# Flamingo block, gated cross attention and MoLE feed-forward: the rest of the values in 32x32 tiles, the last maxima on another engine, the score steps in another order

## The reference

```python
def xattn(query, ctx):                       # 16 heads of 16 channels
    q = (query @ Wq.T + bq) * 16 ** -0.5
    k, v = ctx @ Wk.T + bk, ctx @ Wv.T + bv
    q, k, v = split_heads(q), split_heads(k), split_heads(v)
    k, q = xpos_apply(k, downscale=True), xpos_apply(q, downscale=False)
    w = softmax(einsum('btd,bsd->bts', q, k))          # over 154 keys
    return join_heads(einsum('bts,bsd->btd', w, v)) @ Wo.T + bo

def mole(x, W, b, A, Bm, Rw):                # 3 experts of rank 8
    gates = softmax(x @ Rw)
    return x @ W + b + 1 / 8 * sum_e((x @ A[e]) * gates[e] @ Bm[e])

x = x + tanh(g_xattn) * xattn(layernorm(x), ctx)
x = x + tanh(g_ffn) * mole(relu(mole(layernorm(x), W1, ...)), W2, ...)
```

## Time and profile before

| | |
|---|---|
| median of 3 runs | 531.51 us (530.65 to 532.06) |
| the profiled execution | 530.21 us, of it the span of the trace 528.4 us |
| busy: TensorE / VectorE / ScalarE / GpSimd | 92% / 72% / 39% / 13% |
| mean granted TensorE clock | 0.963 of 2.4 GHz |
| exponentials (L625) | 80 of 1.03 us, 80.6 us |
| values (L1310) and their rest (L1302) | 256 and 64 records on TensorE |

### The profile page before, as it was taken

How to read it: one execution, slowest core, us unless ns; L and a number is a source line. 1 busy time by engine, 2 the same in 40 slices (tenths; PEclk the granted TensorE clock), 3 DMA queues, 4 the chain that set the end, 5 groups by cost and what they waited for, 6 DMA issues and landing times.

```text
span 528.4 us, 7891 instructions
## 1 busy us (share of the span) xinstructions
PE 486.6 (92%) x3032; PEld 353.5 (67%) x3032; DVE 380.0 (72%) x896; ACT 205.3 (39%) x325; POOL 70.5 (13%) x118
## 2 busy tenths in 40 slices
PE   4449939999999999999999999999999999999997
PEld 3335336847876597847876597847876597748796
DVE  4746586958897697958897697958897687925543
ACT  6333522571227412571227412571227412460320
POOL 6363020020202011020202011020202010020000
PEclk9956977999999999999999999999999999999999
DMA  8461140106002140207102140206002040200011
GB/s 320 130 204 43 40 122 2 37 18 190 17 1 82 41 122 1 78 18 186 20 1 82 41 122 1 81 14 189 17 1 82 1 122 1 78 5 1 1 42 40
DMA packets 20385, 34.30 MB, mean 65 GB/s; under 512 B 5588, under 2 KB 9500, under 8 KB 20220
## 3 DMA queue, kind: packets, MB, share of 16 engines
q1 hardware_dynamic: 12704, 16.28, 11.2%
q10 hardware_dynamic: 7644, 17.52, 10.4%
HBM read 14.28 MB, written 4.19 MB: 35 GB/s over the span
## 4 chain that ended last, share of the span: by engine, by line
PE 77%; DVE 14%; ACT 3%; issue 2%; DMA 2%; POOL 1%; SPq 1%; ACTq 0%; DVEq 0%
PE psF L1228 17%; PE psF L1191 13%; PE psX L1211 7%; PE psO L1310 5%; PE psX L1287 4%; PE psX L1118 4%; PE psX L1101 4%; PE psX L1282 4%; PE psF L1302 3%; PE psO L1302 3%; DVE max_t L832 3%; PE psF L1197 3%; DVE xT_lo L765 2%; PE psF L1064 1%; PE psX L1191 1%
## 5 line engine op out<-in xcount | busy, mean ns | idle before, releaser
L832 DVE TENSOR_REDUCE max_t<-psX 128x4 fp32r<-128x616 f32 x128 | 98.9, 795 | 13.1 <-PE psX L1211 11.5
L1211 PE MATMUL psX<-km,qT 128*128 128x308 f32 x256 | 65.6, 346 | 15.8 <-DMA qT<-probs 10.9
L1228 PE MATMUL psF<-w_hi,h_hi 128*128 128x284 f32 (+1 forms) x240 | 72.5, 302 | 0.1
L1228 PE MATMUL psF<-w_lo,h_hi 128*128 128x284 f32 (+1 forms) x240 | 70.3, 293 | 0.0
L1228 PE MATMUL psF<-w_hi,h_lo 128*128 128x284 f32 (+1 forms) x240 | 70.1, 292 | 0.0
L1211 PEld LDWEIGHTS psX<-km,qT 128*128 128x128 f32 x256 | 48.0, 206 | 32.0 <-DVE max_t L832 12.0
L625 ACT ACTIVATE probs<-psX 128x1024 f32<-128x1024 f32 x64 | 64.2, 1025 | 10.9 <-PE psX L1287 10.6
L543 ACT ACTIVATE h_hi<-psF 128x512 fp32r<-128x512 f32 x59 | 34.4, 595 | 55.9 <-PE psF L1197 55.9
L1228 PEld LDWEIGHTS psF<-w_hi,h_hi 128*128 128x128 f32 x240 | 45.1, 188 | 6.0 <-issue 6.0
L402 POOL TENSOR_TENSOR x<-x,tab 128x256 f32<-128x256 f32 x32 | 22.3, 726 | 183.1 <-DMA x<-in_x_dram 183.1
L825 DVE SCALAR_TENSOR_TENSOR h_lo<-psF,h_hi 128x512 fp32r<-128x512 f32 x59 | 39.7, 683 | 8.0 <-ACT h_hi L543 8.0
(11 more groups left out here) (170 smaller groups left out, 881.2 us busy)
## 6 DMA issues: line engine op xcount, KB each, us to landing
qT<-probs SPq DMA_DIRECT2D x32, 256.0 KB
qT<-probs ACTq DMA_DIRECT2D x16, 256.0 KB
x<-in_x_dram ACTq DMA_DIRECT2D x8, 512.0 KB, 3.4
x_ln<-in_x_dram ACTq DMA_DIRECT2D x7, 512.0 KB, 4.1
out_dram<-x ACTq DMA_DIRECT2D x7, 512.0 KB, 2.9
turn<-in_turns_dram SPq DMA_DIRECT2D x2, 512.0 KB, 6.7
heads_t<-in_w_dram SPq DMA_DIRECT2D x1, 1024.0 KB, 8.3
heads_t<-in_w_dram SPq DMA_DIRECT2D x1, 994.0 KB, 7.0
```

Source lines behind the costliest of these rows:

```text
L832: V.tensor_reduce(max_t[:, k, half, :].rearrange("p (h g) -> p g h", h=2)[:, 2 * j:2 * j + 2, :], psX[:, 2 * j:2 * j + 2, 0:2 * S].rearran ...
L1211: ins = mm(psX[:, g % 4, 0:2 * S].rearrange("p (h s) -> p h s", h=2), qT[:, g, tokens(k)], km[:, g, :, 0:S], start=True, stop=True)
L1228: ins = mm(out_bank(d, k)[:, cs], a[:, m, tokens(k)], w[:, m, cs], start=m == 0 and i == 0, stop=m == HT - 1 and i == 2)
```

## The change

- `vr_sb` shrinks from 128 x (4 x 128) to 128 x (4 x 32). `values_rest(c, pair)` now issues eight matmuls of 32 rows x 32 columns: for each of four blocks, the two groups r of the pair, each with its own 32 partitions of `probs_r` and `vr_sb`. `place(r, block)` gives the 32 columns, so that the eight lie in eight different tiles; group 2 pair goes to `psO`, group 2 pair + 1 to a bank of `psF`. The heads are dealt to the groups in another order (`MAIN_PAIRS`, `perm_v` on the host).
- The second rest step of the scores stands fourth (i = 3); both halves of the maxima are waited for by then. `values_rest(c, 0)` waits for four exponentials, part 1 of the values for six.
- `scores(c, 0)` is issued in two halves, with `max_transposed(c, 1)` between. The 16th `max_scores` stands inside `hidden_main(d, 7)`, and VectorE takes the 16th maximum ahead of `h_low(d, 5)`.
- ScalarE copies both halves of the maxima; one DMA for each half.
- `xT_high` stands behind exponential 3 in place of 2, `ctx_copy` behind 6 in place of 4. `project_k` moves from behind score step 7 to behind part 2 of the values, ahead of step 9.
- `project_v` computes for each block of rest values only its own 64 columns.

```diff
-        vr_sb = sb("vr_sb", [P, NQ, P])
+        vr_sb = sb("vr_sb", [P, 4, 32])
...
-                    for hh in range(2):
-                        sp.dma_start(qT[HR * hh + KM:HR * hh + KM + 1, 4 * f:4 * f + 4, :].bitcast(F32),
-                                     max_f[4 * hh:4 * hh + 4, f, :].bitcast(F32)).then_inc(max_rows[f].sem, 16)
+                    sp.dma_start(qT[KM::HR, 4 * f:4 * f + 4, :].bitcast(F32),
+                                 max_f[:, f, :].bitcast(F32)).then_inc(max_rows[f].sem, 16)
...
+                maxima_copy(c, 1)
                 for i, (kind, n) in enumerate(SCORE_STEPS):
...
-                    if i == 2 and not last:
+                    if i == 3 and not last:
                         xT_high(c + 1)
-                    if i == 4 and not last and u == 1:
+                    if i == 6 and not last and u == 1:
                         ctx_copy(b + 1)
...
-                        h_low(d, m)
+                        if m == HT - 2:
+                            h_low(d, m - 1)
+                        if m != HT - 3:
+                            h_low(d, m)
...
-                dve.wait_ge(maxT_ps.sem, maxT_ps.at(c))
-                V.tensor_scalar(max_f[:, 1, :], psO[0:H // 2, :], -1.0, None, ALU.mult).then_inc(maxT_s[1].sem, 1)
...
-                        ins = mm(psF[32 * j:32 * j + SR, 2, E:2 * E], ctxT[:, f, P:S], wkv_sb[:, f, E:2 * E],
+                        o = E + 4 * D * j
+                        ins = mm(psF[32 * j:32 * j + SR, 2, E:E + 4 * D], ctxT[:, f, P:S], wkv_sb[:, f, o:o + 4 * D],
...
+            def place(r, block):
+                return (block + 2 * (r % 2)) % 4
...
-            def values_rest(c, g, first, last):
-                pe.wait_ge(sc_exp.sem, sc_exp.at(c, (1, 1, 6, 6)[g]))
...
-                mm(pv_bank(g), vr_sb[:, g, :], probs_r[:, g, :], start=True, stop=False)
+            def values_rest(c, pair, first, last):
+                pe.wait_ge(sc_exp.sem, sc_exp.at(c, 4))
+                if pair == 1:
+                    pe.wait_ge(pv_t.sem, pv_t.at(c, 1))
...
+                for block in range(4):
+                    for r in (2 * pair, 2 * pair + 1):
+                        j, rows = place(r, block), slice(32 * r, 32 * r + 32)
+                        mm(pv_bank(r)[32 * j:32 * j + 32, :], vr_sb[rows, j, :], probs_r[rows, block, :],
+                           start=pair == 1 or block >= 2, stop=pair == 0 and block < 2)
...
-                pe.wait_ge(sc_exp.sem, sc_exp.at(c, (3, 5, 8, 10)[part]))
+                pe.wait_ge(sc_exp.sem, sc_exp.at(c, (3, 6, 8, 10)[part]))
...
-                scores(c, 0)
+                scores(c, 0, (0, 1))
                 max_transposed(c, 1, first)
+                scores(c, 0, (2, 3))
                 scores(c, 1)
...
                 scores(c, 2)
-                values_rest(c, 0, first, last)
                 scores(c, 3)
-                values_rest(c, 1, first, last)
+                values(c, 0, first)
                 scores(c, 4)
-                values(c, 0)
+                scores(c, 5)
+                values_rest(c, 0, first, last)
+                scores(c, 6)
                 if u == 1 and not last:
                     ctx_transposed(b + 1, ctx_sb)
-                scores(c, 5)
-                scores(c, 6)
                 values(c, 1)
                 scores(c, 7)
+                scores(c, 8)
+                values_rest(c, 1, first, last)
+                values(c, 2)
                 if u == 1 and not last:
                     project_k(b + 1)
-                scores(c, 8)
-                values_rest(c, 3, first, last)
                 scores(c, 9)
-                values_rest(c, 2, first, last)
-                values(c, 2)
...
-SCORE_STEPS = [("rest", 0), ("main", 0), ("main", 2), ("main", 4), ("main", 6),
-               ("rest", 2), ("main", 8), ("main", 10), ("main", 12), ("main", 14)]
+SCORE_STEPS = [("rest", 0), ("main", 0), ("main", 2), ("rest", 2), ("main", 4), ("main", 6),
+               ("main", 8), ("main", 10), ("main", 12), ("main", 14)]
+MAIN_PAIRS = (0, 1, 4, 5, 2, 3, 6, 7)
```

More of the change, by code:

```diff
@@ L218, in build @@
         maxT_ps = count("maxT_ps", 2)
-        maxT_s, max_rows = ([count(f"{n}{f}", per) for f in range(2)] for n, per in (("maxT_s", 1), ("max_rows", 32)))
+        maxT_s, max_rows = ([count(f"{n}{f}", per) for f in range(2)] for n, per in (("maxT_s", 1), ("max_rows", 16)))
         sc_ps, sc_exp = count("sc_ps", 10), count("sc_exp", 10)
@@ L510, in key_constants @@
                     rows = slice(HR * hh, HR * hh + HR)
-                    copy(rest_blocks(rows, hh), one[hh][rows].to_broadcast([HR, NG, SR])).then_inc(kr_init.sem, 1)
+                    copy(rest_blocks(rows), one[hh][rows].to_broadcast([HR, NG, SR])).then_inc(kr_init.sem, 1)
             def key_high(b):
@@ L543, in relu, with maxima_copy @@
                 nc.scalar.activation(h_hi[:, m, :], hidden_bank(d, m), ACT.Relu).then_inc(w1_hi_s.sem, 1)
-            def maxima_copy(c):
-                act.wait_ge(maxT_ps.sem, maxT_ps.at(c, 1))
-                copy(max_f[:, 0, :], psO[0:H // 2, :], scale=-1.0).then_inc(maxT_s[0].sem, 1)
+            def maxima_copy(c, half):
+                act.wait_ge(maxT_ps.sem, maxT_ps.at(c, half + 1))
+                copy(max_f[:, half, :], psO[0:H // 2, :], scale=-1.0).then_inc(maxT_s[half].sem, 1)
             def gate2_exp(e, pr):
@@ L1264, in max_transposed, with scores @@
                 ins.then_inc(maxT_ps.sem, 1)
-            def scores(c, i):
+            def scores(c, i, blocks=range(4)):
                 if i < 2:
@@ L1271, in scores @@
                     pe.wait_ge(sc_exp.sem, sc_exp.at(c, i - 1))
-                if i % 5 == 0:
-                    pe.wait_ge(max_rows[i // 5].sem, max_rows[i // 5].at(c))
+                if i % 3 == 0 and i < 6:
+                    pe.wait_ge(max_rows[i // 3].sem, max_rows[i // 3].at(c))
                 if i == 0:
@@ L1277, in scores @@
                 if kind == "rest":
-                    for k in range(4):
+                    for k in blocks:
                         for hh in range(2):
                             rows = slice(HR * hh, HR * hh + HR)
-                            o = (P + 32) * (2 * n + k) + (-32, 32)[hh] * k
+                            o = (P + 32) * (2 * n + k) - 32 * k
                             ins = mm(psX[:, 2 * (1 - i % 2) + hh, :], kr[rows, o:o + P], qT[rows, 2 * n + k, :],
@@ L1286, in scores, with values @@
                         rows = slice(HR * hh, HR * hh + HR)
-                        ins = mm(psX[:, 2 * (1 - i % 2) + hh, :], km[rows, n // 2, hh, 0:P], qT[rows, n // 2, :],
+                        ins = mm(psX[:, 2 * (1 - i % 2) + hh, :], km[rows, MAIN_PAIRS[n // 2], hh, 0:P],
+                                 qT[rows, MAIN_PAIRS[n // 2], :],
                                  start=True, stop=True)
-                ins.then_inc(sc_ps.sem, 1)
-            def values_rest(c, g, first, last):
-                pe.wait_ge(sc_exp.sem, sc_exp.at(c, (1, 1, 6, 6)[g]))
-                if g == 0:
+                if kind == "main" or blocks[-1] == 3:
+                    ins.then_inc(sc_ps.sem, 1)
+            def place(r, block):
[4 more added lines that the diff above has]
+                    pe.wait_ge(pv_t.sem, pv_t.at(c, 1))
+                    if not last:
+                        pe.wait_ge(xT_lo_s.sem, xT_lo_s.at(c + 1, 1))
+                for block in range(4):
[3 more added lines that the diff above has]
+                           start=pair == 1 or block >= 2, stop=pair == 0 and block < 2)
+            def values(c, part, first=False):
+                pe.wait_ge(sc_exp.sem, sc_exp.at(c, (3, 6, 8, 10)[part]))
+                if part == 0:
                     pe.wait_ge(maxT_s[1].sem, maxT_s[1].at(c))
@@ L1297, in values_rest @@
                         pe.wait_ge(const_v.sem, 2)
-                if g == 2:
-                    pe.wait_ge(pv_t.sem, pv_t.at(c, 1))
-                if g == 3 and not last:
-                    pe.wait_ge(xT_lo_s.sem, xT_lo_s.at(c + 1, 1))
-                mm(pv_bank(g), vr_sb[:, g, :], probs_r[:, g, :], start=True, stop=False)
-            def values(c, part):
-                pe.wait_ge(sc_exp.sem, sc_exp.at(c, (3, 5, 8, 10)[part]))
-                for p in (2 * part, 2 * part + 1):
+                for n in (2 * part, 2 * part + 1):
+                    p = MAIN_PAIRS[n]
                     for hh in range(2):
-                        g, j = 2 * (p // 4) + hh, (p % 4, 3 - p % 4)[hh]
-                        ins = mm(pv_bank(g)[32 * j:32 * j + 32, :], v_sb[:, 4 * g + j, :], probs[:, 2 * (p % 4) + hh, :],
-                                 start=False, stop=True)
+                        r = p % 4
+                        j = place(r, 2 * (p // 4) + hh)
+                        ins = mm(pv_bank(r)[32 * j:32 * j + 32, :], v_sb[:, 4 * r + j, :], probs[:, 2 * (n % 4) + hh, :],
+                                 start=part == 0, stop=part > 0)
```

(3 more changed lines are left out.)

38 lines of the change are left out of this document (21 added, 17 removed).

## The result

The changed kernel takes **526.88 us** (median of 4 runs, 526.69 to 527.12), the kernel before, run beside it, 531.78 (4 runs, 530.65 to 532.37): a ratio of 0.9911, 95% interval 0.9893 to 0.9928. Forecast were 524.9 us, with 521.0 to 530.5 as the range. The span of the trace went from 528.4 to 524.9 us: 3.5 us where the sum of the prediction had 6.6. One execution of a_heads, a kernel of the table further down, took 527.83 us at a lower granted clock than its other three (0.946 for 0.962) and is left out of its median and its ratio.

The account below looks back on a forecast made before the run. TensorE, busy 92% of the span, was taken to bound the kernel, with VectorE's chain close behind. Gains of 3 x 1.2 + 3 x 0.25 + 0.45 + 1.8 = 6.6 us took the median from 531.5 to 524.9 us, range 521.0 to 530.5.

Parts of the forecast that it names:

- A run of eight takes 1.0 us: Rest values on TensorE: two runs of eight matmuls in different tiles, 2.0 us a chunk for 4.2, 2.2 saved.
- the slower rival: Rest values: row groups go in turn, a run of eight takes 1.9 us, kernel 6.2 us slower at 537.7; 10%.
- The new order of an even chunk: TensorE from score step 0: step 3 at 3.85, `project_q` at 12.8 us against 14.5, a gain of 1.7.
- VectorE lets 1.2 of 1.7 through: Chunks 2, 4, 6: `q_products` at 15.13 against 16.30, so VectorE's chain gains 1.2 us of TensorE's 1.7.
- Odd chunks 0.25 each: Chunks 1, 3, 5: later `project_k` and keys delay VectorE, TensorE waits over 1 us, 0.25 us of gain passes.
- the maxima land late: Rival at step 3: maxima land 3.0 us after issue, step 3 starts 0.8 later, 531.2 us, no change; 12%.
- Chunk 0, the failed term: First chunk: the last part of the values waits about 0.65 us for exponential 9, leaving a gain of 0.45 us.
- something else: Remaining rival, such as the clock's half-rate stretch after chunk 0 ending earlier or later, 1 to 2 us; 4%.
- The tail, counted at nothing: Span behind the last transposes of x2, the feed-forward input: forecast change 0.
- Last chunk 1.8: Last chunk: VectorE's chain hangs on the last part of the values, so TensorE's gain of 1.8 us counts.
- At nothing: Items given no gain: VectorE's dropped copy, earlier 16th maximum, `h_low` order, fewer DMA issues, later `xT_high`, `project_v`.

Follow-up runs that it names:

- a_heads: The changed kernel with ScalarE copying the high half of the first two groups of heads ahead of exponential 9 instead of behind it; 519.73 us.
- b_keys: The changed kernel with `project_k` back between score steps 7 and 8, the heads' copy still behind exponential 9; 523.57 us.
- c_both: The changed kernel with the heads' copy ahead of exponential 9 and `project_k` back between score steps 7 and 8; 519.57 us.
- z_ctx: x_step9k with the two DMAs of the next context, in odd chunks, issued behind exponential 1 instead of ahead of the second maxima's copy; 519.49 us.
- x_step9: The changed kernel with score step 9 issued ahead of values 2 and `project_k`, no work removed; 525.44 us.
- x_step9k: x_step9 with `project_k` also back between score steps 7 and 8; 519.84 us.
- h_order: The changed kernel with VectorE's old order of the last maxima and `h_low`; 526.99 us.

## Why the prediction was right, and where not

- **A run of eight takes 1.0 us**: 1.02. Right, and so the slower rival falls with it, at its own point of decision (1.5 us).
- **The new order of an even chunk**: step 3 at 3.77 (3.85), `project_q` at 12.83 (12.8), exponential 9 at 12.94 (12.86), `q_products` at 15.13 (15.13). Right but for what step 3 waits for: the prediction had it wait for a DMA that lands 2.2 us after its issue. The DMA took 1.80 and had landed, and exponential 1 ended last, at 3.72 where 3.65 was forecast. That the two lay 0.1 to 0.2 us apart made the number come out.
- **VectorE lets 1.2 of 1.7 through**: 1.21, 1.25 and 1.16. Right, and shown by the experiments: freeing the chain in two independent ways gives the same 0.5 back, and 1 us of TensorE's work counts whole ahead of step 9 and half behind it.
- **Odd chunks 0.25 each**: 0.74, 0.39 and -0.38. That the mean is 0.25 is luck: chunk 1 has 1.0 us less at half rate than before, and chunks 3 and 5 together gain nothing. The mechanism is right in the main (keys late, a new wait at `lora2_operand` of 0.98 us in all three; it stays at 0.97 to 0.99 in b_keys, falls to 0.4 in a_heads and is gone in c_both, so it takes both edits to undo it), and chunk 3 follows it, with `q_products` at 18.28 (18.5). What was missed is step 3 of odd chunks, where ScalarE's copy starts 0.3 us late, behind the two DMA issues of the next context, and above all the landing in chunk 5, 2.62 us after the issue where 2.2 was taken; `q_products` stood at 19.09 there. It is the rival "the maxima land late", come true in one chunk of seven. z_ctx, which moves the context, takes most of the lateness away; whether the context or the packet of instructions beside it brought it on is open.
- **Chunk 0, the failed term**: -0.45 forecast, +1.22 measured. Its last part of the values waited 1.12 us for exponential 9, not 0.65, which is 0.5 of the 1.7:

```profile
62.77 0.62 PE L1324 MATMUL psO<-probs,v_sb 128*32 128x512 f32 x2 [1.12 <-ACT probs L624]
```

  x_step9, x_step9k and z_ctx, which bring step 9 forward, take 1.0 us off this chunk. The rest goes for the most part with the half-rate clock behind step 0, 5.8 us of it for 2.4 up to `project_q`, where 1.2 us less is worth 0.5 in b_keys. The prediction had this as "something else", 1 to 2 us.
- **The tail, counted at nothing**: +1.5, a half-rate stretch where the kernel before had none. No step of the sum had it.
- **Last chunk 1.8**: 1.89. **At nothing**: h_order confirms the order of the maxima; `project_v` was not tried alone.

The range held. The forecast was 2 us low, and that it was no more is in part luck: between the traces the gain falls 3.1 us short of the sum (3.5 for 6.6), nearly all of it at the two ends, but the traced execution of the kernel before was 1.3 us under its median and that of the changed kernel only 0.2.

## What to carry to other kernels

When work is taken from the busiest engine, ask for each piece of it whether it stands ahead of or behind the operation from which the next engine's chain starts: here a microsecond ahead of step 9 counts whole, behind it half or not at all. Then look at what stands in front of that chain's first link in the helper engine's queue: here one 0.6 us copy behind one exponential was worth 0.5 us in each even chunk and 0.8 in each odd one, 3.1 us in five chunks, where the whole change had brought 4.9. A transfer that becomes needed earlier needs its own look at everything issued just ahead of it, in every kind of iteration.
